# TensorE's second-stage products regrouped, the output norm's weight moved into the projection, and mean squares from VectorE's statistics

## What is computed

```python
# branch 1: Mamba-2 block and MLP
z, xBC, dt = split(layernorm(xn) @ in_proj.T)
xs, Bm, Cm = split(silu(causal_conv4(xBC)))
y = scan(xs, dt, A, Bm, Cm) + xs * D
y = y * silu(z)
y = y * rsqrt(mean(y ** 2) + EPS) * norm_w
x = xn + y @ out_proj.T
x = x + gelu(layernorm(x) @ w1.T + b1) @ w2.T + b2
# branch 2: causal attention with 16 heads of 8 channels, and 4 experts (2 per token)
g = silu(attention_and_experts(xn))
out = residual + x * g
```

## Time and profile before

| what | value |
|---|---|
| median of 3 runs | 864.25 us |
| profiled execution, its own time | 864.34 us |
| its span | 862.6 us |
| TensorE's granted clock, mean | 0.993 |
| one round in the middle of the loop | 100.9 us |
| of it stage_a from step 2 on | 40.7 us |

### The profile page before, as it was taken

One profiled execution on the slowest core, in us unless ns is written; L12 is line 12 of the kernel. 1 busy time (PEld: TensorE's weight loads), 2 busy tenths in 40 slices (PEclk: granted clock), 3 DMA queues, 4 the chain that ended last, 5 costly groups with the idle time before them and its releaser, 6 DMA issues. The chain is left out here.

```text
span 862.6 us, 18148 instructions
## 1 busy us (share of the span) xinstructions
PE 788.2 (91%) x5472; PEld 483.5 (56%) x5472; DVE 610.4 (71%) x1467; ACT 502.4 (58%) x960; POOL 318.7 (37%) x600
## 2 busy tenths in 40 slices
PE   2779999999999989999999999999999998999897
PEld 1455564756556555655647565475556556475555
DVE  2786479784888758785697848877587866968534
ACT  2435784467753776457844677537765577446652
POOL 5424534053512617045340534226260362505400
PEclk9998999999999999999999999999999999999999
DMA  4000000000000000000000000001000000000000
GB/s 166 2 8 14 14 2 1 9 16 25 0 8 12 26 0 0 8 13 25 0 0 8 14 24 0 2 14 30 1 0 8 12 26 0 0 8 14 25 1 13
DMA packets 15145, 11.73 MB, mean 14 GB/s; under 512 B 1040, under 2 KB 13968, under 8 KB 14992
## 3 DMA queue, kind: packets, MB, share of 16 engines
q1 hardware_dynamic: 15120, 11.43, 4.4%
HBM read 7.76 MB, written 2.10 MB: 11 GB/s over the span
## 5 line engine op out<-in xcount | busy, mean ns | idle before, releaser
L1099 ACT ACTIVATE sb_pr<-S 128x768 f32<-128x768 f32 (+1 forms) x192 | 165.9, 891 | 129.7 <-PE S L444 129.7
L1196 DVE TENSOR_REDUCE sb_mx<-S 128x2 f32<-128x256 f32 (+3 forms) x256 | 198.0, 817 | 29.7 <-PE S L444 29.3
L1716 POOL TENSOR_SCALAR_AFFINE_SELECT sb_pr<-sb_pr 128x256 f32<-128x256 f32 (+1 forms) x192 | 98.9, 517 | 322.2 <-ACT sb_pr L1099 319.7
L444 PE MATMUL R<-sb_pr,sb_va 128*32 128x512 f32 (+3 forms) x1024 | 89.5, 444 | 0.0
L444 PE MATMUL R<-sb_W,sb_pr 128*128 128x96 f32 (+1 forms) x512 | 69.5, 276 | 0.0
L444 PE MATMUL R<-sb_xfT,sb_W 128*128 128x512 f32 x144 | 69.2, 602 | 0.0
L444 PE MATMUL S<-sb_kT,sb_qT 32*128 32x256 f32 (+3 forms) x512 | 56.3, 384 | 13.7 <-DVE sb_mx L1196 10.0
L444 PEld LDWEIGHTS R<-sb_W,sb_pr 128*128 128x128 f32 x512 | 63.5, 192 | 3.8 <-issue 3.5
L444 PEld LDWEIGHTS S<-sb_kT,sb_qT 32*128 32x128 f32 x512 | 27.5, 183 | 66.3 <-DVE sb_mx L1196 58.6
L444 PE MATMUL S<-sb_qT,sb_kT 32*128 32x256 f32 (+3 forms) x512 | 56.3, 384 | 5.7 <-ACT sb_pr L1099 4.9
L1430 DVE SCALAR_TENSOR_TENSOR sb_x<-R,sb_wts,sb_x 128x96 f32<-128x96 f32 x128 | 40.6, 317 | 22.8 <-PE R L444 19.4
(11 more groups left out here) (216 smaller groups left out, 1735.6 us busy)
## 6 DMA issues: line engine op xcount, KB each, us to landing
sb_xin<-x SPq DMA_DIRECT2D x9, 256.0 KB, 2.7
sb_W<-weights SPq DMA_DIRECT2D x1, 2290.0 KB, 11.0
sb_qT<-sb_mT SPq DMA_DIRECT2D x128, 4.0 KB
sb_xres<-x SPq DMA_DIRECT2D x8, 256.0 KB, 2.8
out<-sb_xres SPq DMA_DIRECT2D x7, 256.0 KB, 2.3
sb_cT<-sb_xact SPq DMA_DIRECT2D x8, 128.0 KB, 2.3
sb_W<-weights SPq DMA_DIRECT2D x1, 514.0 KB, 5.8
sb_cst<-consts SPq DMA_DIRECT2D x1, 328.0 KB, 3.1
```

Of the source, the lines that this page charges most:

```text
L444: return pe.matmul(o, lhsT, rhs, start=start, stop=stop, skip_group_check=True)
L1099: act.activation(pr[:, e % 4, :, 0:n], S[pair_of_exp(e)][:, :, 0:n], ACT.Exp).then_inc(p_sb, 1)
L1196: o = dve.tensor_reduce(mx[:, n // P - 1, g, heads[0]:heads[1] + 1], found[:, :, at_col:at_col + n], AX.X, ALU.max, negate=True)
L1716: pool.affine_select(out=keep, in_=keep, compare_op=ALU.is_ge, fill=0.0, base=0, pattern=pattern, channel_multiplier=-1)\
```

## The change

1. **Order on TensorE.** In quarters 1 to 3 each `exp_scores_of_four` is followed at once by one `weigh_values`, and the 128*128 products stand together behind it. `weigh_values(20)` of quarter 3 now comes ahead of `scan_outputs(3)`, and `prep_a` behind it. `turn_maxima` of the second pair goes to (1, 0) and bank R[3]. In `scan_outputs` the wait for `wm` stands ahead of the products that use it.
2. **Order on ScalarE, VectorE and GpSimd to match.** `evac_values` stands at u = 0, `evac_y` at u = 1, the exponential of the segments at u = 3; VectorE's `values` and `scan_products` at u = 2 and `scan_weights` at u = 3; GpSimd's `xw` at u = 3. `SIGMOID_AT` 9 becomes 11, `JOIN_AT` 11 and 15 become 15 and 17, `STATS_AT` 8 becomes 9.
3. **Mean squares.** `square_y` on ScalarE goes. VectorE takes statistics of each `yz` (one `bn_stats` of 256 columns per chunk), and behind the last chunk four `bn_aggr` and two tiny `tensor_tensor` make mean squares of them.
4. **Norm weight.** VectorE multiplies the output projection's weights by `norm_w` once, ahead of the first stage_a; `evac_y` is one plain copy of 256 columns.

```diff
-SIGMOID_AT = {5: (0, 1, 2), 9: (3, 4)}
-JOIN_AT = {11: (0, 1), 15: (2,)}
+SIGMOID_AT = {5: (0, 1, 2), 11: (3, 4)}
+JOIN_AT = {15: (0, 1), 17: (2,)}
-STATS_AT = 8
+STATS_AT = 9
...
             def turn_values(r, g):
...
+                if g == 0:
+                    pe.wait_ge(mT_sb, at(mT_sb, r, 2))
...
-                    if u == 0 and g > 0:
-                        turn_y(r, g - 1)
-                    if u == 1 and g > 0:
-                        weigh_values(r, e - 3)
-                        segments(r, g)
-                        scan_inputs(r, g)
                     if e == 2:
                         segments(r, 0)
-                    if u == 3:
-                        weigh_values(r, e - 3)
-                        if g >= 1:
-                            turn_values(r, g - 1)
+                    if u == 0 and g > 0:
+                        weigh_values(r, e - 2)
+                        turn_y(r, g - 1)
+                        if g == 1:
+                            turn_maxima(r, 1, R[3])
+                        segments(r, g)
+                    if g == 0 and u == 3:
+                        weigh_values(r, 0)
+                    if u == 2 and g > 0:
+                        weigh_values(r, e - 2)
+                        turn_values(r, g - 1)
+                        scan_inputs(r, g)
                     if u == 4:
+                        if g > 0:
+                            weigh_values(r, e - 2)
                         scan_outputs(r, g)
-                    if u == 5:
-                        if g < T - 1:
+                        if g == T - 1:
+                            prep_a(r)
+                        elif g > 0:
                             new_state(r, g)
-                        weigh_values(r, e - 3)
-                    if (g, u) == (1, 2):
-                        turn_maxima(r, 1, R[1])
-                    if (g, u) == (3, 3):
-                        prep_a(r)
+                    if g == 0 and u == 5:
+                        new_state(r, 0)
+                        weigh_values(r, 2)
...
-                for n in range(2):
-                    i = act.activation(yT[:, n, c * P:(c + 1) * P], R[2][:, n * P:(n + 1) * P], ACT.Copy,
-                                       scale=vec[:, V_NORM + n:V_NORM + n + 1])
-                i.then_inc(yT_sb, 1)
+                act.activation(yT[:, :, c * P:(c + 1) * P], R[2][:, 0:DI].rearrange("p (n t) -> p n t", n=2),
+                               ACT.Copy).then_inc(yT_sb, 1)
...
+            def square_sum(r, c):
+
+                dve.wait_ge(yz_sb, at(yz_sb, r, c + 1))
+                i = dve.bn_stats(yst[:, c, :], yz[:, c % 2, :])
+                if c == T - 1:
+                    i.then_inc(yst_sb, 1)
+                    dve.wait_ge(yst_sb, at(yst_sb, r, 1))
+                    dve.sem_inc(dve_passed, 1)
+                    for t in range(T):
+                        i = dve.bn_aggr(ymv[:, t, :], yst[:, t, :])
+                    i.then_inc(yst_sb, 1)
+                    dve.wait_ge(yst_sb, at(yst_sb, r, 2))
+                    dve.wait_ge(ry_sb, at(ry_sb, r, 1))
+                    tt(yss[:, 0], ymv[:, :, 0], ymv[:, :, 0], ALU.mult).then_inc(yss_sb, 1)
+                    dve.wait_ge(yss_sb, at(yss_sb, r, 1))
+                    tt(yss[:, 1], yss[:, 0], ymv[:, :, 1], ALU.add).then_inc(yss_sb, 1)
...
+            dve.wait_ge(wt_loaded, 16)
+            for n in range(2):
+                ts(w2("op", D)[:, n, :], w2("op", D)[:, n, :], vcol(V_NORM + n), None,
+                   ALU.mult).then_inc(op_scaled, 1)
```

More of the change, by code:

```diff
@@ L190, in build @@
         junk = sb("junk", [P, 2, DI])
-        yss = sb("yss", [P, T])
+        yst = sb("yst", [P, T, 6])
+        ymv = sb("ymv", [P, T, 2])
+        yss = sb("yss", [P, 2, T])
         ry = sb("ry", [P, 3, T])
@@ L231, in build @@
         wt_loaded = signal("wt_loaded", 0)
+        op_scaled = signal("op_scaled", 0)
         x_loaded = signal("x_loaded", 16, 1)
@@ L308, in build @@
         oT_sb = signal("oT_sb", G)
-        yss_sb = signal("yss_sb", T)
+        yst_sb = signal("yst_sb", 2)
+        yss_sb = signal("yss_sb", 2)
         yT_sb = signal("yT_sb", T)
@@ L501, in turn_maxima @@
                 if pair:
-                    pe.wait_ge(seg_sb, at(seg_sb, r, 2))
+                    pe.wait_ge(yz_sb, at(yz_sb, r, 1))
                 for t in range(T):
@@ L598, in scan_outputs @@
                 s = slice(c * P, (c + 1) * P)
-                pe.wait_ge(wm_sb, at(wm_sb, r, c + 1))
                 pe.wait_ge(xdt_sb, at(xdt_sb, r, c + 1))
@@ L608, in scan_outputs @@
                     mm(R[3][:, n * P:(n + 1) * P], xact[:, n, s], diag_d[:, n, :], c == 0 and n == 0, False)
+                pe.wait_ge(wm_sb, at(wm_sb, r, c + 1))
                 for h in range(NH):
@@ L617, in new_state @@
                 pe.wait_ge(seg_sb, at(seg_sb, r, c + 1))
-                if c == 1:
-                    pe.wait_ge(mT_sb, at(mT_sb, r, 2))
                 mm(R[1][0:NS, 0:DI], btok[:, c % 2, :], xw[:, c % 2, :]).then_inc(hn_ps, 1)
@@ L904, in _ @@
             pe.wait_ge(wt_loaded, 16)
+            pe.wait_ge(op_scaled, 2)
             with pe.Fori(0, B - 1) as r:
@@ L988, in stage_b @@
                     act.wait_ge(x1_sb, at(x1_sb, r, 0))
-                    inverse_root(r, yss[:], ry, ry_sb, 1.0 / DI, 0)
+                    inverse_root(r, yss[:, 1], ry, ry_sb, 1.0, 0)
                 if head:
@@ L1013, in stage_b @@
                     act.wait_ge(x2_sb, at(x2_sb, r, 2))
-                    act.wait_ge(yss_sb, at(yss_sb, r, 0))
                     for t in range(T):
@@ L1105, in negative_exp @@
                 act.activation(gs[:], x2[:], ACT.Exp, scale=-1.0).then_inc(gs_sb, 1)
-            def square_y(r, c):
-                act.wait_ge(yz_sb, at(yz_sb, r, c + 1))
-                act.wait_ge(ry_sb, at(ry_sb, r, 1))
-                act.wait_ge(yss_sb, at(yss_sb, r, c - 1))
-                act.wait_ge(x2ss_sb, at(x2ss_sb, r, 1))
-                act.activation(junk[:, c % 2, :], yz[:, c % 2, :], ACT.Square,
-                               accum_out=yss[:, c:c + 1]).then_inc(yss_sb, 1)
             def stage_a(r, tail):
@@ L1127, in stage_a @@
                     if u == 0 and g > 0:
+                        evac_values(r, g - 1)
+                    if u == 1 and g > 0:
                         evac_y(r, g - 1)
-                    if u == 1 and g > 0:
-                        evac_values(r, g - 1)
-                    if u == (2 if g == 0 else 1):
+                        if g == 1:
+                            evac_maxima(r, 1, R[3])
+                    if u == (2 if g == 0 else 3):
                         act.wait_ge(seg_ps, at(seg_ps, r, g + 1))
@@ L1135, in stage_a @@
                                        ACT.Exp).then_inc(seg_sb, 1)
-                    if u == 1 and g > 0:
-                        square_y(r, g - 1)
-                    if (g, u) == (1, 2):
-                        evac_maxima(r, 1, R[1])
                     if e == 3 and tail:
                         negative_exp(r)
-                    if (g, u) == (3, 3):
+                    if (g, u) == (3, 5):
                         evac_a(r)
@@ L1145, in stage_a @@
                 evac_y(r, T - 1)
-                square_y(r, T - 1)
                 evac_values(r, G - 1)
@@ L1483, in scan_combine @@
                 dve.wait_ge(yT_ps, at(yT_ps, r, c - 1))
-                dve.wait_ge(yss_sb, at(yss_sb, r, c - 1))
                 if c == 0:
@@ L1519, in stage_a @@
                             split_maxima(r, MAX_AT[e] // UNITS)
-                    if u == 1:
+                    if u == 2 and g >= 1:
+                        values(r, g - 1, ot_ps, ao_sb)
+                    if u == (2 if g else 1):
                         scan_products(r, g)
-                    if u == 2:
+                    if u == (3 if g else 2):
                         scan_weights(r, g)
-                    if u == 3 and g >= 1:
-                        values(r, g - 1, ot_ps, ao_sb)
                     if u == 5 and g < T - 1:
                         scan_state(r, g)
+                    if u == 5:
+                        square_sum(r, g)
                     for t in XN_AT.get(e, ()):
@@ L1718, in stage_a @@
                         .then_inc(pm_sb, 1)
-                    if u == 2 and g < T - 1:
+                    if u == (3 if g else 2) and g < T - 1:
                         pool.wait_ge(xdt_sb, at(xdt_sb, r, g + 1))
```

## The result

The changed kernel takes 873.74 us (median of 18 runs, 872.09 to 881.01), the kernel before 864.17 us in the same session (18 runs). Ratio 1.0097, 95% interval 1.0076 to 1.0118. The profiled execution takes 872.56 us with a span of 870.8 us, against 864.34 and 862.6. The forecast was 870.1 us, range 860 to 875, so the time lies in the range: 2.5 us above the forecast by the profiled executions, 3.6 by the median. The median is also 0.7 above the forecast's own narrower range of 867 to 873.

What follows compares the result with a forecast made beforehand. TensorE, busy 91% of the span, was taken as the bound, other engines mattering only where it waits. From 864.34 us, -1.9 for order, tail and other parts and +7.7 for the collision gave 870.1 us, range 860 to 875.

Steps and rivals of the forecast that it cites:

- Quarters 1 and 2: Stage_a's quarters 1 and 2, without collisions: both shrink to 9.41 us, by 0.85 and 0.09.
- The tail: End of quarter 3: a W now ahead of scan_outputs makes the last turn_y 0.70 us later each round.
- The collision: Two-input VectorE joins and GpSimd exclude each other: quarter 3's W behind S(2) 1.1 us late in 7 stages, +7.7 us.
- the third join holds GpSimd up for some 0.25 more: Start of quarter 3: the moved third join delays GpSimd's next select by 0.25 us, from 3.66 to 3.9.
- The stretch of 2.62 us behind the selects: GpSimd's time from one select's end to the next's start, including the 1.86 us power; assumed unchanged at 2.62.
- The statistics: VectorE's bn_stats lie in its idle time and the chain after the last yz runs beside other work: 0.
- The weights: Two one-time products scaling the projection weights, and a wait for a load: between 0 and 1.4 us, taken as 0.
- The signs: Right if quarters 1 and 2 take 9.4, W waits 0.5 or more, selects and joins exceed 0.8, turn_y waits over 1.
- a stage_b of another length: Listed as a sign that the forecast is wrong: stage_b's length differing from before; no size given.
- No exclusion: Rival: joins and GpSimd do not exclude each other where it matters; 862.4 us, chance 0.27.
- Faster: Rival: GpSimd in time, and VectorE or ScalarE at stage_b's start takes the tail's 0.70 back; 856.8 us, chance 0.10.
- The heavier collision: Rival: VectorE is held up too, so S(2) moves and W(2) is 1.9 us late; 875.7 us, chance 0.13.

Runs made afterwards that it cites:

- e8: Changed kernel with mean squares back on ScalarE and evac_y again multiplying by norm_w in two instructions; 870.74 us, ratio 1.0040.
- e4: Kernel before, in its old order, with both the mean squares from VectorE's statistics and the norm weight in the projection; 861.95 us, ratio 0.9943.
- e11: Kernel before with only the norm weight scaled into the projection and the plain evac_y; 860.17 us, ratio 0.9949.
- e2: Changed kernel with the first two joins replaced by one-input VectorE reductions of about the same length, gating products left out; 869.41 us, ratio 1.0023.
- e7: Changed kernel with only the joins moved, the first two to e = 11 and the third to e = 21; 865.11 us, ratio 0.9971.
- e10: Kernel before with only the joins moved to the changed kernel's places, e = 15 and e = 17; 866.40 us, ratio 1.0012.
- e12: Kernel before with only the mean squares taken from VectorE's statistics, evac_y still in two instructions with norm_w; 862.73 us, ratio 0.9959.
- e13: Kernel before with the norm weight in the projection, the plain evac_y and the new order in quarter 1 alone; 864.92 us, ratio 1.0010.

## Why the prediction was right, and where its sizes were off

**Quarters 1 and 2** (-0.85 and -0.09): measured -0.86 and -0.10. S(4) stands at 5.74 to 5.75 behind S(0), forecast 5.75. That the savings of ScalarE buy nothing beside the new order is shown by e8; that this is a property of the order, and not of the savings, by e4 and e11, which the prediction had not said.

**The tail** (+0.70): 0.67 in the first stage, with turn_y waiting 0.99 for `yz`.

**The collision** (+1.1 in 7 stages): the mechanism is shown by e2 (one input less: 0.99 back), e7 (joins away: 1.33 back) and `yc` beside `yz` in e10. Its size was 1.33, just at the end of its bounds of 0 to 1.3 (1.30 against the kernel before). The chain of the working held up to the selects: their end was forecast 1.04 behind S(0), and is 503.80 - 502.70 = 1.10. The step that failed is "the third join holds GpSimd up for some 0.25 more". It is 0.54 (0.74 - 0.20), since `bn_stats` moved that join; without it, in e8, it is 0.21. A part of this was hidden by luck. The stretch of 2.62 us behind the selects was taken over with the power at 1.86, and 0.22 of that is the same exclusion: there `yz` (499.18) starts just ahead of the power (499.24). In the changed kernel the power starts first and takes 1.64.

**The statistics** (0): that is the term that was mis-sized. I looked for their price in VectorE's idle time and behind the last `yz`. There they cost nothing. I did not ask whom the instruction behind them would meet. Price 0.32 a round in this order. It is contained in the 1.33: without it, in e8, the W is 4.63 - 3.62 = 1.01 late, close to the 1.1 of the forecast.

**The weights** (0): quarter by quarter 0. But the first stage_b of the loop (from the projection's start to ScalarE's first instruction of stage_a) is 53.63 us instead of 52.56, in all eight profiled kernels that have parts 3 and 4 together, and in none of those without both (before, e8, e10, e11, e12, e13). Most of it, 0.80, is the same exclusion in a third place. GpSimd, and VectorE, which builds the experts' gates, in the changed kernel:

```profile
140.94 1.04 POOL L1715 TENSOR_TENSOR sb_rs<-sb_cst,sb_dta 128x512 f32<-128x512 f32 x1 [0.16 <-POOL sb_dta L1706]
```

```profile
137.69 2.35 DVE L1189 TENSOR_REDUCE sb_mx<-S 128x2 f32<-128x1024 f32 x2 [0.19 <-issue]
...
141.02 1.03 DVE L1275 TENSOR_TENSOR sb_gq<-sb_gq,sb_cst 128x64 f32<-128x64 f32 x1
```

Sixty-four columns that take 0.23 in the next round take 1.03 behind `rs`, and TensorE waits 1.20 us for the maxima behind them, where it waits 0.31 in the next round. The other 0.25 comes ahead of that: VectorE stands idle before the reduction at 137.69 (0.19, and the profile shows nobody that it waits for), which starts 30.88 behind the projection's start instead of 30.63. This also changes who comes first behind it. In the next round a VectorE instruction with two inputs from SBUF (`cv`) starts ahead of GpSimd's `dt` and holds it to 0.66; here `dt` comes first, takes 0.22, and `rs` starts 0.30 earlier, ahead of the 64 columns. All eight kernels have this idle time and this order, and the six others have neither. Why VectorE stands idle there is open; neither part alone does it (e11, e12).

**The sum.** Forecast +5.8 in the profiled executions, measured +8.2. The missing 2.4 are 7 x 0.23 of the collision and 1.07 once, less 0.2 of the tail. What the first stage gains goes into a later start: the first projection starts at 106.8 in both profiles. Both hold one stretch of low clock that costs 1.4 us (see the last section), which cancels.

**The signs.** Quarters of 9.4, a W that waits 0.75 for the select, long joins and selects, and a first stage whose quarters 1 to 3 are 0.36 shorter came as named. The last turn_y waits 0.99 for `yz`, just under the "over 1 us" of the list. One sign of being wrong came too: a stage_b of another length, the first one.

**The rivals.** No exclusion: fell by e2 and e7. Faster: fell, since stage_b keeps its 52.56 from the second round on and the tail's 0.67 goes through (e7: last turn_y at 10.33, with everything else in time). The heavier collision is half there: VectorE is held up as well (a join of 1.52), segments wait 0.31 for the state and S(2) stands at 3.75 instead of 3.04. But the W is 1.30 late and not 1.9.

## What to carry to other kernels

A small instruction moved to a free place is not free if it reads two operands from SBUF on VectorE while GpSimd works: write down which two-input VectorE instructions lie beside which GpSimd instructions that TensorE waits for, and price them one behind the other, in the new order and not in the old. Price an edit in the order in which it will stand: the joins' new step was free in the old order and cost 1.33 us in the new one, and ScalarE's savings were worth 0.6 us a round in the old order and nothing in the new one. Distances measured in different kernels can't be put together quarter by quarter (e13), unless what one quarter hands to the next comes at the same time.
